# The passage from an 8-head into a 16-head attention: latents and first projections moved among the last heads, expert sums on GpSimd, row maxima subtracted with 64-row matmuls

## The chip, the cores and the metric

The kernel runs on one core of a Trainium2 chip. The time is device microseconds of the whole program, median of three runs, inputs in the chip's main memory at the start and the output there at the end. TensorE (PE) multiplies, VectorE (DVE), ScalarE (ACT) and GpSimd (POOL) do the elementwise work; each engine works off its own queue in order and they wait for one another on semaphores. Matrix products land in eight PSUM banks of 128 partitions by 512 floats; POOL does not touch them here.

## The reference, cut to what matters

```python
x = x + tanh(g_xattn[0]) * mlstm(layernorm(x), ctx)      # B=4, S=256, D=128
x = x + tanh(g_ffn[0]) * switch_head(layernorm(x))       # x2: 8 heads, 5 experts, 64 wide
x = x + tanh(g_xattn[1]) * L1_xattn(ctx, mask, layernorm(x))   # x3: 16 heads, 64 wide
x = x + tanh(g_ffn[1]) * experts(x)                      # 8 experts, best one

# end of switch_head: out is (b, t, 8, 64), md chooses 3 of 5 experts per head
o5 = einsum("bthd,dm->bthm", out, Wo).reshape(b, t, 8, 5, 128)
y = einsum("bthem,bthe->btm", o5, md)

# L1_xattn(features, masks, latents)
lat = layernorm(latents); kv = concat([layernorm(features), lat], 1)
q = lat @ Wq; k = kv @ Wk; v = kv @ Wv                    # 16 heads of 64, 512 keys
sim = (q * 64**-0.5) @ k.T; sim = sim - max(sim)
out = softmax(where(mask, sim, -inf)) @ v @ Wo
```

The kernel gathers `out` by expert first (`z`, 5 x 64 = 320 wide, the sum over heads of head output times md), and multiplies `z` by Wo: that gives x2. Latents are x2, normalized twice (once by the call, once inside).

## The kernel before

A batch is 256 rows, two tiles of 128; heads of the 8-head attention run in `pe_b`, `act_b`, `dve_b`, `pool_b`, heads of the 16-head attention in `pe_c`, `act_c`, `dve_c`, `pool_c`. A number is split into a high and a low fp16 half for most products, so a projection is three matmuls (high by high, high by low, low by high), the high half copied by ACT, the remainder subtracted by VectorE.

The 8-head attention has 12 steps per batch (`STEPS`), one head started in each of steps 0 to 7; steps 5 to 11 of batch b run in a loop together with the projections of batch b+1 (`Fori(0, B - 1)`). For the last batch steps 5 to 11 stand alone at the end. There `dve_b` adds statistics and norms of the latents of batches 0 to 2 (`latent_stats`, `latent_norm`, L688, L1851, L1855); then `copies_z` makes ten products of 512 (L775), POOL adds tile 0 over heads (L868 to L870) and VectorE tile 1 (L825 to L827), PE turns and multiplies z (L1712, L550), ACT copies it (L641, L642) and `add_x2` (L781) ends the stage. `latent_low` (L697, L699) and `latent_high` (L670) split the latents between. POOL meanwhile splits weight chunks (L1676 high, L1678 low).

The 16-head attention has 32 steps (`STEPS_C`), eight pairs of heads for each of four batches; a loop covers 24 of them. Step t on PE: `scores_T(t, 0)` (L1034, six pairs of 64-row matmuls of 256 columns; L1041 subtracts the maxima with a 128-row identity), `row_max(t+1, 0)` (L1019), job c, `scores_T(t, 1)`, `row_max(t+1, 1)`, jobs f and h, `values(t-1)` (48 matmuls, L1059 to L1061), and in two steps of a batch `project_ao` (L1067). ACT: the exponentials of a step (L1159 full, L1160 high half), job c's high copy after the first pair, f's and h's at the end (L1144). VectorE: `take_max` (L1250) for both halves with job c between, job f (L1241 for K), `take_out` (L1268, L1271), job h (L1239 for V). POOL: `low_exps` (L1361).

Jobs are the projections ahead: q in every other step at place c (L1244 its remainder), the turning of the finished output (ao) at c otherwise, K at f (L950 to L952), V at h. They take two PSUM banks in turns: a job waits until the job two before it is freed. `BEFORE` is the list of jobs ahead of step 0, `AFTER` the one behind step 31. The scores of a pair use banks 2 to 5; row maxima take banks 6 and 7, values and output bank 6 too:

```python
if n >= 2:
    pe.wait_ge(s.c_pj_free, it * PJ + (n - 1))          # job: two banks
...
if p >= 3:
    pe.wait_ge(s.c_O_free, it * HP2 + (p - 2))          # row_max(p, 0)
...
pe.wait_ge(s.c_max_done, it * PAIRS + (2 * t + 4))      # values(t-1) in step t
```

## Time and profile before

| | |
|---|---|
| time, median of 3 runs (lowest to highest) | 764.17 us (761.3 to 765.28) |
| profiled execution: time, span | 763.59 us, 761.9 us |
| busy, share of the span: PE, DVE, ACT, POOL | 80%, 75%, 43%, 55% |
| mean granted clock of TensorE | 0.880 |
| PE busy in tenths, slices 18 to 24 of 40 (19 us each, from 343 us) | 8 4 2 8 9 9 9 |
| chain that ended last | PE 57%, DVE 28%, issue 7%, ACT 3%, POOL 3% |

The shares are means over stages with different limits. What matters for a change in one stage are three views: the table of stretches (which engine is full there, and at which clock), the chain of waits in that stretch (which work ends last, piece by piece), and the timelines of the engines (how long one instruction takes, what it waited for; an idle time and its releaser stand in brackets).

### The profile page before, as it was taken

What the parts mean: (1) busy time and instruction counts of PE and PEld (TensorE: products, weight loads), DVE (VectorE), ACT (ScalarE), POOL (GpSimd) and SP (SyncE); (2) the same over time, 40 slices, a digit from 0 to 9 for tenths busy, and PEclk for the clock granted to TensorE, in tenths of its full rate; (3) what the DMA queues carried; (4) which work ended last, traced back from release to release, by engine and by line L of the source; (5) the groups of instructions that cost most, each with busy time, mean ns of one, the idle gap of its engine ahead of it and who ended that gap; (6) DMA issues with size and microseconds to landing.
All of it is one profiled execution on the core that took longest, in us unless ns stands there. A gap on an engine that the chain in (4) does not pass through costs nothing.

```text
span 761.9 us, 15577 instructions
## 1 busy us (share of the span) xinstructions
PE 610.9 (80%) x5721; PEld 387.8 (51%) x5721; DVE 569.0 (75%) x1043; ACT 324.3 (43%) x565; POOL 417.5 (55%) x349
## 2 busy tenths in 40 slices
PE   6399756798468658838428899999999998799997
PEld 5277522354244335325313456666666665566766
DVE  4837899659969985995976777667667766489887
ACT  2433200231132132113213787767858766455661
POOL 5424254417636652769593756656656666346652
PEclk9999977769779858965556999999999999989999
DMA  7311100000000000003310000000000000000001
GB/s 190 90 34 29 55 1 0 0 2 1 0 2 0 0 0 0 0 0 97 96 28 0 2 2 2 2 2 2 2 2 2 2 2 2 1 1 0 0 0 28
DMA packets 14163, 12.95 MB, mean 17 GB/s; under 512 B 3120, under 2 KB 11936, under 8 KB 14112
## 3 DMA queue, kind: packets, MB, share of 16 engines
q1 hardware_dynamic: 14112, 12.25, 5.6%
q8 instruction: 35, 0.57, 0.3%
q14 instruction: 16, 0.13, 0.1%
HBM read 11.72 MB, written 0.52 MB: 16 GB/s over the span
## 4 chain that ended last, share of the span: by engine, by line
PE 57%; DVE 28%; issue 7%; ACT 3%; POOL 3%; DVEq 1%; DMA 1%; ACTq 0%; SPq 0%; POOLq 0%; PEld 0%
DVE work L717 5%; PE banks L1034 5%; PE banks L1712 5%; DVE work L775 4%; PE banks L1041 4%; PE banks L950 3%; PE banks L465 3%; PE banks L1059 3%; PE banks L1019 2%; PE banks L952 2%; PE banks L951 2%; PE banks L1067 2%; PE banks L1422 2%; PE banks L1061 2%; PE banks L1060 2%
## 5 line engine op out<-in xcount | busy, mean ns | idle before, releaser
L1361 POOL TENSOR_TENSOR attn<-work,attn 128x512 f16<-128x512 f32 (+1 forms) x96 | 141.9, 1481 | 94.8 <-ACT attn L1160 94.8
L1250 DVE TENSOR_REDUCE nmax<-banks 128x2 bf16<-128x1024 f32 x64 | 78.3, 1223 | 21.5 <-PE banks L1019 21.3
L717 DVE TENSOR_TENSOR work<-banks,gatev 128x512 f32<-128x512 f32 x120 | 79.3, 684 | 15.8 <-PE banks L467 15.3
L465 PE MATMUL banks<-weights,xbTh 128*128 128x512 f16 x120 | 50.7, 422 | 28.2 <-DVE work L717 26.7
L1469 POOL TENSOR_SCALAR work<-work 128x512 f16<-128x512 f32 x64 | 53.0, 851 | 35.7 <-ACT work L1401 33.1
L1159 ACT ACTIVATE work<-banks,maskbias 128x512 f32<-128x512 f32 x64 | 44.3, 692 | 59.7 <-PE banks L1041 59.7
L845 POOL TENSOR_TENSOR work<-work 128x512 f32<-128x512 f32 x24 | 30.5, 1269 | 66.6 <-DVE work L717 64.6
L1407 DVE TENSOR_TENSOR work<-work 128x512 f16<-128x512 f32 x64 | 57.1, 949 | 12.2 <-POOL work L1469 12.2
L1712 PE MATMUL banks<-ident,work 128*128 128x128 f32 x276 | 53.3, 331 | 8.5 <-DVE work L1912 3.0
L490 PE MATMUL banks<-attn 64*128 64x256 f16 x64 | 22.1, 360 | 47.0 <-ACT work L631 37.9
L1059 PEld LDWEIGHTS banks<-work,attn 128*128 128x128 f16 x512 | 46.8, 97 | 18.8 <-POOL attn L1361 10.8
L1059 PE MATMUL banks<-work,attn 128*128 128x65 f16 x512 | 49.8, 193 | 5.2 <-DVE work L1271 2.5
L631 ACT ACTIVATE work<-banks,nm 128x256 f32<-128x256 f32 x64 | 26.7, 471 | 62.9 <-DVE nm L742 62.9
L1061 PE MATMUL banks<-work,attn 128*128 128x65 f16 x512 | 49.9, 193 | 0.0
L1060 PE MATMUL banks<-work,attn 128*128 128x65 f16 x512 | 49.9, 194 | 0.0
L466 PE MATMUL banks<-weights,xbTh 128*128 128x512 f16 x120 | 49.8, 415 | 0.0
L467 PE MATMUL banks<-weights,xbTl 128*128 128x512 f16 x120 | 49.8, 415 | 0.0
L1241 DVE TENSOR_TENSOR k2l<-banks,k2h 128x512 f16<-128x512 f32 x32 | 22.1, 692 | 36.0 <-ACT k2h L1144 36.0
L1712 PEld LDWEIGHTS banks<-ident,work 128*128 128x128 f32 x276 | 38.6, 170 | 19.6 <-issue 7.5
L1401 ACT ACTIVATE work<-banks,b1T 128x512 f32<-128x512 f32 x64 | 40.4, 688 | 15.6 <-PE banks L1395 15.5
L1061 PEld LDWEIGHTS banks<-work,attn 128*128 128x128 f16 x512 | 46.8, 98 | 0.0
L1060 PEld LDWEIGHTS banks<-work,attn 128*128 128x128 f16 x512 | 46.8, 97 | 0.0
(275 smaller groups left out, 1922.2 us busy)
## 6 DMA issues: line engine op xcount, KB each, us to landing
stage<-in_L_ffn_w SPq DMA_DIRECT2D x8, 512.0 KB, 3.9
stage<-in_L_ffn_Wkv SPq DMA_DIRECT2D x4, 640.0 KB, 3.9
stage<-in_L_ffn_Wq SPq DMA_DIRECT2D x2, 640.0 KB, 5.1
xt<-in_x SPq DMA_DIRECT2D x1, 512.0 KB, 4.2
ct<-in_ctx SPq DMA_DIRECT2D x1, 512.0 KB, 5.5
wo<-in_L_xattn_Wo SPq DMA_DIRECT2D x1, 512.0 KB
stage<-in_L_xattn_Wv SPq DMA_DIRECT2D x1, 512.0 KB, 3.7
stage<-in_L_xattn_Wq SPq DMA_DIRECT2D x1, 512.0 KB, 3.5
```

The lines of the kernel that those rows point to most:

```text
L465: pe.matmul(o, xh, wh, start=True, stop=False)
L466: pe.matmul(o, xh, wl, start=False, stop=False)
L467: pe.matmul(o, xl, wh, start=False, stop=True).then_inc(s.pj_ready, 1)
L717: dve.tensor_tensor(heads8(m.prod[:, k, e, :]), heads8(bank_pj[c % 2][:, :]), wide(g, DH1), ALU.mult).then_inc(s.prod_ready, 1)
L1059: pe.matmul(o, ph, vh, start=(kt == 0), stop=False)
L1060: pe.matmul(o, ph, vl, start=False, stop=False)
L1061: ins = pe.matmul(o, pl, vh, start=False, stop=(kt == KT - 1))
L1250: dve.tensor_reduce(m.nmax[:, p % 2, i, :], banks[:, 6:8, :], AX.X, ALU.max, negate=True).then_inc(s.c_max_done, 1)
L1361: pool.tensor_tensor(m.Pl[:, p % 2, kts, :], m.Pf[:, kts, :], m.Ph[:, p % 2, kts, :], ALU.subtract).then_inc(s.c_P_lo, 1)
L1407: dve.tensor_tensor(m.hTl[:, a, f, :], m.hf[:, use % HR, :], m.hTh[:, a, f, :], ALU.subtract).then_inc(s.h_lo, 1)
L1469: pool.tensor_scalar(m.hTh[:, use // FT, use % FT, :], m.hf[:, use % HR, :], 1.0, 0.0, ALU.mult, ALU.add).then_inc(s.h_hi, 1)
L1712: return pe.transpose(dst, src, m.ident[0:src.shape[0], 0:src.shape[0]])
```

## The change

- The loops of the 16-head attention are written out; `PJ` is 0 and a table `pj_no` counts the jobs.
- In `dve_b` the ten products and the sums of the last batch go. POOL makes them head by head (`z_head`): one product of both tiles and five experts, 640 elements, and one addition of 640, for heads 0 to 3 behind the batch loop and for heads 4 to 7 at steps 0, 2, 4 and 6.
- z of the last batch becomes ring jobs at place g: turned at steps 8 and 10 (zt), multiplied at 9 and 11 (zw), where VectorE adds x2.
- Latents are made batch by batch. Batch 0: statistics and norms behind head steps 5 to 7 of the last batch, its transposes are the first of the jobs `BEFORE`, which stand at head steps 8 to 11 (`TAIL`). Batches 1, 2, 3: statistics from steps 0, 4, 12, turned at g of steps 3, 7, 15, each with its valid keys behind.
- V tiles 0 and 1 of batch 0 are jobs at g of step 0 and at e of step 1. Order of the places is c, e, f, h, g.
- POOL's splits of w1 and w2 (eight chunks) go to steps 14 to 29, one half per step.
- The maxima are subtracted with 64-row matmuls of 128 columns in two passes; the second follows `row_max` and a wait for the first, and gives S_ready.

The diff, cut to its core:

```diff
+        def latent_stats(dve, stats, b, k):
+
+            if k == 0:
+                dve.wait_ge(s.x2_ready, I + b * I + I)
             else:
-                dve.wait_ge(s.x2n_ready, k)
-            src = m.ct if k % 2 else m.xt
-            stats(lambda t: src[:, tiles[t], :], len(tiles), m.st, m.mv, s.x2_var)
-
-        def latent_norm(dve, batches, k):
-            tiles = range(batches[0] * I, (batches[-1] + 1) * I)
-            src = m.ct if k % 2 else m.xt
-            dve.wait_ge(s.x2_var, k + 1)
-            dve.wait_ge(s.x2_rstd, k + 1)
-            for t in range(len(tiles)):
-                ins = dve.tensor_scalar(m.ct[:, tiles[t], :], src[:, tiles[t], :], m.mv[:, t, 0:1], m.rs[:, t:t + 1], ALU.subtract, ALU.mult)
...
-            z_group = SUMS + (B - 1) * GROUPS
-            for i in range(I):
-                copies_z(B - 1, i, z_group + i)
-
-            dve.wait_ge(s.z_ready, B * I)
-            t = m.prod[:, 1, :, :].rearrange("p e (h c) -> p e h c", h=H1)
-            ch.link(dve.tensor_tensor(t[:, :, 0:4, :], t[:, :, 0:4, :], t[:, :, 4:8, :], ALU.add))
-            ch.link(dve.tensor_tensor(t[:, :, 0:2, :], t[:, :, 0:2, :], t[:, :, 2:4, :], ALU.add))
-            dve.tensor_tensor(m.z[:, 1, :].rearrange("p (e c) -> p e c", e=E1), t[:, :, 0, :], t[:, :, 1, :], ALU.add).then_inc(s.z_last, 1)
...
+            def z_head(h):
+                if h == 0:
+                    pool.wait_ge(s.zT_ready, (B - 1) * I)
+                if h % 2 == 0:
+                    pool.wait_ge(s.O_free, (B - 1) * O1 + (h // 2 + 1 + RING))
+                heads = m.ho[:, :, h * DH1:(h + 1) * DH1].unsqueeze(2).to_broadcast([P, I, E1, DH1])
+                md = m.topm[:, (B - 1) * I:B * I, G1 + h * E1:G1 + (h + 1) * E1].unsqueeze(3).to_broadcast([P, I, E1, DH1])
+                dst = (m.z_head if h else m.z)[:, :, :].rearrange("p i (e c) -> p i e c", e=E1)
+                ch.link(pool.tensor_tensor(dst, heads, md, ALU.mult))
+                if h:
+                    ins = pool.tensor_tensor(m.z[:, :, :], m.z[:, :, :], m.z_head[:, :, :], ALU.add)
+                    if h < H1 - 1:
+                        ch.link(ins)
+                    else:
+                        ins.then_inc(s.z_sum, 1)
...
+            latent_rstd(0)
+            z_head(0)
+            latent_rstd(1)
+            for h in range(1, 4):
+                z_head(h)
+            return latent_rstd, z_head
...
+        PLACES = "cefhg"
+        LATENTS = {1: (0, 3), 2: (4, 7), 3: (12, 15)}
+        Z_AT = 8
...
+            if t < I:
+                jobs["ge"[t]] = ("v", 0, t, 0)
+            if Z_AT <= t < Z_AT + 4:
+                jobs["g"] = (("zt", "zw")[(t - Z_AT) % 2], B - 1, (t - Z_AT) // 2)
+            for lb, (_, at) in LATENTS.items():
+                if t == at:
+                    jobs["g"] = ("lat", lb)
...
-        BEFORE = [("q", 0, 0), ("v", 0, I, 0), ("k", 0, 0), ("k", 0, 1)] + [("v", 0, a, 0) for a in range(I)]
+        BEFORE = [("lat", 0), ("q", 0, 0), ("v", 0, I, 0), ("k", 0, 0), ("k", 0, 1)]
+        TAIL = {8: (0,), 9: (1,), 10: (2, 3), 11: (4,)}
...
+                elif kind == "zt":
+                    _, b, i = j
+                    pe.wait_ge(s.z_sum, b * I + 1)
+                    for c in range(3):
+                        w = min(P, E1 * DH1 - c * P)
+                        ins = turn(bank[0:w, c * P:(c + 1) * P], m.z[:, i, c * P:c * P + w])
+                    ins.then_inc(s.zT_ready, 1)
+                    return
...
-                for h in range(2):
-                    o = pair[h][:, :].rearrange("p (k i c) -> p k i c", k=2, i=I)
-                    for i in range(I):
-                        less = m.nmax[:, p % 2, i, h:h + 1].to_broadcast([P, P])
-                        ins = pe.matmul(o[:, :, i, :], less, m.identb[:, :].unsqueeze(1).to_broadcast([P, 2, P]), start=False, stop=(i == I - 1))
-                ins.then_inc(s.c_S_ready, 1)
+                less_max(p, half, 0)
...
+            def less_max(p, half, x):
+
+                pair = bank_kq[2 * half:2 * half + 2]
+                for i in range(I):
+                    for h in range(2):
+                        g = (x + h) % 2
+                        r = slice(DH2 * g, DH2 * g + DH2)
+                        o = pair[h][:, :].rearrange("p (k i c) -> p k i c", k=2, i=I)[:, :, i, r]
+                        ins = pe.matmul(o, m.nmax[r, p % 2, i, h:h + 1].to_broadcast([DH2, P]),
+                                        m.identb[r, r].unsqueeze(1).to_broadcast([DH2, 2, DH2]), start=False, stop=(x == 1 and i == I - 1))
+                        if x == 0 and i == I - 1:
+                            ins.then_inc(s.c_less_done, 1)
+                return ins
+
+            def rest_of_max(it, p, half):
+
+                pe.wait_ge(s.c_less_done, 2 * (it * PAIRS + (2 * p + half + 1)))
+                less_max(p, half, 1).then_inc(s.c_S_ready, 1)
...
                 scores_T(it, t, 0)
                 if t + 1 < STEPS_C:
                     row_max(it, t + 1, 0)
+                rest_of_max(it, t, 0)
                 if "c" in jobs:
                     job(it, (t, "c"), jobs["c"])
                 scores_T(it, t, 1)
                 if t + 1 < STEPS_C:
                     row_max(it, t + 1, 1)
-                for place in "fh":
+                rest_of_max(it, t, 1)
+                for place in "efhg":
...
+            def before(ps):
+                for p in ps:
+                    if p == 0:
+                        pe.wait_ge(s.x2_ready, I + (B - 1) * I)
+                        for n in range(N_W0, N_W1):
+                            pe.wait_ge(s.w_split, n + 1)
+                        pe.wait_ge(s.kv_free, 2)
+                    job(0, (-1, p), BEFORE[p])
...
+                if kind == "zt":
+                    dve.wait_ge(s.zT_copied, j[1] * I + (j[2] + 1))
+                    dve.wait_ge(s.c_pj_free, n)
+                    dve.sem_inc(s.c_pj_free, 1)
+                    return
...
+                for place in "hg":
+                    if place in jobs:
+                        low(it, (t, place), jobs[place])
+                for lb, (at, _) in LATENTS.items():
+                    if t in (at + 1, at + 2):
+                        latent_norm(dve, lb, t - at - 1)
+                    if t in (at, at + 1):
+                        latent_stats(dve, stats, lb, t - at)
...
+            tail[5] = lambda: latent_stats(dve, stats, 0, 0)
+
+            def second():
+                latent_norm(dve, 0, 0)
+                latent_stats(dve, stats, 0, 1)
+            tail[6] = second
+            tail[7] = lambda: latent_norm(dve, 0, 1)
...
+                if t in (0, 2, 4, 6):
+                    z_head(4 + t // 2)
+                if t == SPLITS_AT:
+                    pool.wait_ge(s.pj_ready, B * X1)
+                if SPLITS_AT <= t < SPLITS_AT + 2 * (N_WALL - N_W1):
+                    n, half = divmod(t - SPLITS_AT, 2)
+                    (split_low if half else split_high)(N_W1 + n)
```

## Rows read from the trace of the kernel before

**Rows 1.** Stretches: busy us (instructions) of PE, PEld, DVE, ACT, POOL; clock; DMA; GB/s.
```profile
180.00:200.00 20.00, 14.45 (x97) 7.18 (x97) 18.89 (x34) 2.28 (x4) 13.49 (x11) 1.00 0.00 1
340.00:360.00 20.00, 14.88 (x79) 10.25 (x79) 10.64 (x13) 6.22 (x17) 19.18 (x12) 0.50 0.25 79
...
380.00:400.00 20.00, 4.11 (x14) 2.75 (x14) 15.70 (x17) 1.94 (x6) 17.93 (x11) 0.50 0.10 27
...
460.00:480.00 20.00, 19.96 (x282) 12.47 (x280) 14.17 (x21) 16.19 (x27) 13.03 (x9) 1.00 0.01 2
```
**Rows 2.** Chain that ended last, 320 to 420 us: start, us, what.
```profile
378.08 6.12 DVE work L775 x10
384.22 4.06 DVE work L825
```
**Rows 3.** Timeline of VectorE: start us, us, engine, line, operation, out<-in, count [idle before <-releaser].
```profile
358.93 0.35 DVE L781 SCALAR_TENSOR_TENSOR xt<-banks,gf,xt 128x128 f32 x1 [3.06 <-PE banks L550]
...
373.36 4.06 DVE L688 TENSOR_SCALAR ct<-ct,mv,rs 128x128 f32<-128x128 f32 x6 [0.15 <-POOL rs L1648]
...
403.31 2.34 DVE L1256 COPY_PREDICATED kvTl<-masked,kvTl 128x256 f16<-128x256 uint8 x1
```
**Rows 4.** Timeline of ACT, the first exponential of the 16-head attention.
```profile
416.11 0.69 ACT L1159 ACTIVATE work<-banks,maskbias 128x512 f32<-128x512 f32 x1 [1.07 <-PE banks L1041]
```
**Rows 5.** Timeline of TensorE: the first scores of steps 0, 8 and 16.
```profile
414.33 0.39 PE L1034 MATMUL banks<-q2h,k2h 64*128 64x256 f16 x2
...
471.94 0.28 PE L1034 MATMUL banks<-q2h,k2h 64*128 64x256 f16 x2
...
531.24 0.28 PE L1034 MATMUL banks<-q2h,k2h 64*128 64x256 f16 x2
```
**Rows 6.** Timeline of POOL: sums over heads of a loop batch and of the last, a split.
```profile
342.94 1.86 POOL L869 TENSOR_TENSOR work<-work 128x640 f32<-128x640 f32 x1
...
359.29 1.04 POOL L1676 TENSOR_SCALAR weights<-stage 128x1024 f16<-128x1024 f32 x1
...
381.26 5.67 POOL L868 TENSOR_TENSOR work<-work 128x1280 f32<-128x1280 f32 x1 [4.68 <-DVE work L775]
```
**Rows 7.** Timeline of TensorE in one step, and the change L1019 to L1034 in step 30.
```profile
500.05 0.19 PE L1059 MATMUL banks<-work,attn 128*128 128x65 f16 x1
500.08 0.19 PE L1060 MATMUL banks<-work,attn 128*128 128x65 f16 x1
...
502.15 0.27 PE L1034 MATMUL banks<-q2l,k2h 64*128 64x256 f16 x2
502.35 0.61 PE L1041 MATMUL banks<-identb,nmax 128*128 128x256 bf16 x4
502.90 0.39 PE L1019 MATMUL banks<-k2h,q2h 64*128 64x512 f16 x2
503.22 0.28 PE L950 MATMUL banks<-kvTh,wq1h 128*128 128x256 f16 x1
...
637.25 0.39 PE L1019 MATMUL banks<-k2h,q2h 64*128 64x512 f16 x2
637.47 0.27 PE L1034 MATMUL banks<-q2h,k2h 64*128 64x256 f16 x2
```
**Rows 8.** Timeline of ACT: a step with an ao job (first two), one with a q job.
```profile
496.14 0.69 ACT L1159 ACTIVATE work<-banks,maskbias 128x512 f32<-128x512 f32 x1 [3.19 <-PE banks L1041]
...
500.24 0.64 ACT L1144 ACTIVATE k2h<-banks 128x512 f16<-128x512 f32 x1
...
503.00 0.69 ACT L1159 ACTIVATE work<-banks,maskbias 128x512 f32<-128x512 f32 x1 [1.64 <-PE banks L1041]
...
507.58 0.64 ACT L1144 ACTIVATE k2h<-banks 128x512 f16<-128x512 f32 x1
```
**Rows 9.** Timeline of VectorE: K's remainder, then take_out.
```profile
492.49 0.69 DVE L1241 TENSOR_TENSOR k2l<-banks,k2h 128x512 f16<-128x512 f32 x1 [1.32 <-ACT k2h L1144]
...
493.30 0.42 DVE L1271 TENSOR_TENSOR work<-banks,den 128x256 f32<-128x256 f32 x1
```

More of the change, by code:

```diff
@@ L661, in act_b @@
                 step(B - 1, h, False)
-                if h == STEPS - 1:
-                    for b in range(B - 1):
-                        latent_high(act, b)
-            for i in range(I):
-                copy_z(B - 1, i)
+                if h in tail:
+                    tail[h]()
         def latent_high(act, b):
@@ L932, in build @@
         for t in range(STEPS_C):
-            ordered += [((t, p), j) for p, j in c_jobs(t).items()]
+            ordered += [((t, p), j) for p, j in sorted(c_jobs(t).items(), key=lambda pj: PLACES.index(pj[0]))]
         ordered += [((STEPS_C, p), j) for p, j in enumerate(AFTER)]
         for place, j in ordered:
-            hi_no[place] = sum(1 for p in job_no if dict(ordered)[p][0] not in ("ao", "lat"))
+            hi_no[place] = sum(1 for p in job_no if dict(ordered)[p][0] in ("q", "k", "v", "norm"))
             job_no[place] = len(job_no)
@@ L940, in build @@
             if j[0] == "v":
-                v_no[j[1] * 2 + j[3]] = job_no[place]
-        PJ, PJ_HI = 3 * HP2, 3 * HP2 - 2 * I
-        for t in range(SPLIT_AT, STEPS_C - HP2 - 3):
-            assert all(job_no[t + HP2, p] == job_no[t, p] + PJ and hi_no[t + HP2, p] == hi_no[t, p] + PJ_HI for p in "cfh")
+                v_no[j[1] * 2 + j[3]] = max(job_no[place], v_no.get(j[1] * 2 + j[3], 0))
+        PJ, PJ_HI = 0, 0
+        pj_no = {place: sum(1 for q, j in ordered if job_no[q] < job_no[place] and j[0] not in ("zt", "zw")) for place in job_no}
         N_JOBS = len(job_no)
@@ L1281, in step @@
                     take_max(it, t + 1, 1)
-                if "f" in jobs:
-                    low(it, (t, "f"), jobs["f"])
+                for place in "ef":
+                    if place in jobs:
+                        low(it, (t, place), jobs[place])
                 if t >= 1:
@@ L1309, in dve_c @@
-            for it in range(B - 1):
-                for t in range(SPLIT_AT, SPLIT_AT + HP2):
-                    step(it, t)
-            for t in range(STEPS_C - HP2 + SPLIT_AT, STEPS_C):
+                for place in "hg":
+                    if place in jobs:
+                        low(it, (t, place), jobs[place])
+                for lb, (at, _) in LATENTS.items():
[3 more added lines that the diff above has]
+                        latent_stats(dve, stats, lb, t - at)
@@ new lines, in before @@
+            def before(ps):
+                for p in ps:
+                    if p == 0:
+                        dve.wait_ge(s.maskb_ready, 1)
+                        dve.wait_ge(s.v2_ones, 1)
+                        dve.wait_ge(s.tanh_ready, 1)
+                    low(0, (-1, p), BEFORE[p])
+            tail = {h: (lambda ps=ps: before(ps)) for h, ps in TAIL.items()}
+            tail[5] = lambda: latent_stats(dve, stats, 0, 0)
+            def second():
+                latent_norm(dve, 0, 0)
+                latent_stats(dve, stats, 0, 1)
@@ L1313, in dve_c, with run, attend16_dve @@
+            tail[6] = second
+            tail[7] = lambda: latent_norm(dve, 0, 1)
+            def run():
+                attend16_dve(dve, ch, norm, norm_stats, take_max, step, take_out, low, low_norm, add_x3)
+            return tail, run
+        def attend16_dve(dve, ch, norm, norm_stats, take_max, step, take_out, low, low_norm, add_x3):
+            dve.sem_inc(s.h_lo, HR)
+            for i in range(I):
+                take_max(0, 0, i)
+            for t in range(STEPS_C):
                 if t == STEPS_C - 1:
```

265 lines of the change are left out of this document (113 added, 152 removed).

## Prediction, made before any run of the changed kernel

> **What bounds the kernel now.** The view of stretches comes first, since the change lies between two stages with different limits. In the steady part of the 16-head attention TensorE is busy for 19.96 of 20 us at full clock [rows 1]; in the passage ahead of it TensorE works 4.11 of 20 us at half clock while VectorE is busy for 15.70 [rows 1]. The chain of waits, read second, says what the passage costs: it goes from work on VectorE to work on VectorE, through the ten products L775 and the sums from L825 on [rows 2], not through TensorE. The timelines give the rest. Last x2 of the batch loop at 358.93 [rows 3], first exponential of the 16-head attention at 416.11 [rows 4]: 57.2 us of passage. Then 32 steps of TensorE: step 0 starts at 414.33, step 8 at 471.94, step 16 at 531.24 [rows 5], so 57.6 us for steps 0 to 7 and 59.3 us for a batch of 8 later. The profiled execution took 763.59 us, 1.7 us over its span of 761.9, and lies 0.6 us under the median of 764.17; I work from 763.6.
>
> **Part 1, the passage.** Removed from it: ten products (6.12 us) and the first sum of tile 1 (4.06 us) with two smaller ones on VectorE [rows 2], three latents and two x2, after which the valid keys end only at 405.65 [rows 3], and the first projections behind them. The products and sums become 15 POOL instructions of 640 elements; L869, 640 elements wide, took 1.86 us [rows 6], so up to 3.6 us per head. They run beside the last heads and steps 0 to 6. What is late next is batch 0's own latent chain. From row to row (pieces without a group are my estimates from the same timelines, to 0.3 us each): VectorE ends head step 5 at 361.0 as now; statistics of two tiles 0.9 = 362.0; POOL's two instructions 1.1 = 363.1; norm and second statistics with head step 6's own work between, 2.5 = 365.6; head step 7, 1.9 = 367.5; last norm 1.4 (0.7 each beside POOL, L688 4.06 for six [rows 3]) = 368.9; transposes 0.8 = 369.7; latent_low with ACT's half 2.1 = 371.8; valid keys and head step 9 on VectorE 3.7 = 375.5 (one copy of them took 2.34 beside POOL's splits [rows 3], and POOL is now never idle there); low q, then V, K0 and K1, each three 512-column matmuls at half clock, about 1.3 us, plus copy and remainder on a ring of two banks = 381.2; two row maxima and the first scores 4.2 = 385.4. Against 416.1 that is **30.7 us won**. Ends: 34 (SBUF work of VectorE undisturbed by POOL) and 21 (every such instruction of POOL and VectorE stretched as at 381.26, where 1280 elements took 5.67 instead of 2.88 us [rows 6]). I take 30.7, since L699 and L1256 did stretch beside the splits and ops on PSUM did not. V tiles 0 and 1 are not removed but moved into steps 0 and 1.
>
> **Part 2, the maxima.** Each half of a step subtracts them now with four 256-column matmuls, one each 0.11 us, and around them lie changes between 64-row and 128-row work: L1034 ends and L1041 starts 0.20 us after the last pair instead of 0.11, L1019 to L950 is 0.32 for 0.213 of columns, while L1019 to L1034, both 64 rows, is 0.22 [rows 7]. So a change of row mode costs 0.09 to 0.11 us. The new form has eight 128-column matmuls in pairs: columns 0.44 to 0.22 per half and four changes of mode fewer per step. On TensorE that is 0.43 + 0.4 = 0.8 us per step. I don't take it, because TensorE would then no longer be the bound. What follows it is a chain that the change itself closes: S_ready is now given by rest_of_max, which stands *behind* row_max(t+1, 0) on TensorE, and that waits for take_out. Chain of a step: first exponential to the copy of K on ACT 4.58 us with a q job (503.00 to 507.58) or 4.10 with an ao job (496.14 to 500.24) [rows 8]; to its remainder L1241, 0.66; remainder to the end of take_out 1.23 (492.49 to 493.72) [rows 9]; then 0.06 to TensorE, row_max 0.213, rest_of_max 0.11 and 0.21 to its end and ACT. Sum 7.06 (q) and 6.58 (ao). Now these steps take 7.05 and 6.85. Steps with project_ao stay with TensorE: 8.91 now, 8.48 after (only columns and modes ahead of L1067 count). A batch of eight: 2 x 7.06 + 4 x 6.58 + 2 x 8.48 = 57.4 against 59.3: **1.9 us won per batch**, 3.8 for steps 16 to 31. Ends: 12.8 (0.8 in each of 16 steps, no chain) and a loss of 4.8 (0.3 per step, if the new wait shows). That wait is rest_of_max's for c_less_done; behind it on TensorE stand the c job and the second scores. It is covered by row_max, 0.213 us of columns, against the 0.2 us that a short matmul needs to its end (L1059, 0.19 [rows 7]); without that cover it costs up to 0.15.
>
> The Trainium skill has a rule against this part: TensorE: Matmul & The Clock Gate, LDWEIGHTS (loading the stationary operand), says that a load costs by its columns, not by its rows, some 107 ns for 128, so that eight loads of 64 rows cost twice four loads of 128. By it each half would cost 0.4 us more, not less. The trace doesn't bear it out here: L1059 and L1060, each with a 128-column load, follow at 0.03 us [rows 7].
>
> **Part 3, ring jobs.** The ring of projections has two banks, and job n waits until job n-2 is freed. With c, f, h that never hurts: h waits for c. A fourth job (g, or e at step 1) waits for f, the K projection. K's copy stands behind all exponentials on ACT, and its remainder ends 5.93 us after the first exponential (q) or 5.45 (ao). g stands ahead of values on TensorE, so values, scores and row_max wait. Counted from row_max0 (0.53 us before the first exponential): g starts at 6.52 or 6.04, then its own columns (zt 0.35, zw 0.65, lat 0.25, V 0.65), then 1.54 for values and 0.78 to the next row_max0 (1.87 more with project_ao). Steps: zt in q 9.2, zt with project_ao 11.1, zw in ao 9.0, lat 8.6, V at step 0 8.0 (no values) and 9.4 at step 1. There are nine of them: 0, 1, 3, 7, 8, 9, 10, 11, 15. Latents cost VectorE too: statistics and norm stand behind take_out and delay the next take_max0, 0.6 us per full pair and 0.4 otherwise; latent_low blocks ACT and VectorE after steps 3, 7 and 15, 1.4 us each. The z jobs add two waits on VectorE, for ACT's copy of zT and for the x2 it just wrote, with the next take_max0 behind; ACT has copied 1.2 us before that one is due, so nothing. Sum of steps 0 to 7: 8.0 + 9.4 + 7.7 + 8.7 + 8.5 + 7.0 + 7.7 + 8.7 = 65.7, against 57.6. Steps 8 to 15: 10.6 + 9.0 + 11.1 + 9.0 + 8.5 + 7.0 + 7.7 + 8.7 = 71.6 against 59.3. **Lost: 8.1 + 12.3 + 1.4 (step 16) = 21.8 us.** Bounds: zero, if K is freed before V's columns end, and 27, if all nine wait 0.6 us more. I take the rows' sum, since every link of it is a duration of the trace.
>
> POOL's splits of w1 and w2 go to steps 14 to 29: 1.04 us for a high half [rows 6] and twice that for a low one, beside 4.4 us of low_exps in steps of over 6.5; z_head, 3.6 us in every other step, fits in two steps too (8.9 + 3.6 + 1 under 14). Cover gone, each would cost about 1 us where it is late. Unrolled loops cost nothing: the steps outside the loop run at the same spacing. TensorE is idle in short pieces to 385, so step 0 runs at half clock longer than now; I add 1 us.
>
> Sum: 763.6 - 30.7 + 21.8 - 3.8 + 1 = 751.9.
>
> **Rivals.**
> A, forecast: 752, own range 743 to 760.
> B, the fourth job doesn't stop the ring: the nine waits (about 20 us together) go. 732, between 725 and 742. For it: TensorE waits nowhere for the ring now; against it: the order of the jobs in the code.
> C, TensorE's own rate rules, nothing waits: 763.6 - 30.7 - 32 x 0.8 + 6 of moved jobs = 713. Against it: ACT is busy 16.19 of 20 us [rows 1] and its chain has no slack for 0.8. The Trainium skill, TensorEngine Tiling (Array Packing), Key Properties, says that changing the tiling mode drains the engine, and by that rule alone C would come out; the 0.1 us of rows 7 agrees with the rule, not with the result.
> D, slower: TensorE's clock falls in steps 0 to 15. They leave TensorE idle for 2 us or more each, and 14.88 us of work in 20 stood at 0.50 once, though 14.45 stood at 1.00 elsewhere [rows 1]. At half clock values, scores, maxima and the extra job on the path cost some 2.3 us more per step: 16 steps give 37, so 788; it is slower from about six such steps on.
> E, the passage is stretched by POOL (z_head and VectorE at the slow end): 30.7 becomes 21, 762.
> F, loads set the pace of the 64-row maxima: 0.3 us per step on the chain, 32 steps, 762.
>
> **How the numbers follow.** A 0.50, B 0.20, C 0.06, D 0.10, E 0.08, F 0.06. Predicted 752. The range 729 to 767 holds A, E, F and most of B. 0.5% (3.8 us) is about what a measurement of this kernel can tell from no change. Faster by over that: A, B, C and a part of E and F, 0.78; within: the rest of E, F and A's upper tail, 0.12; slower: D, 0.10.
>
> **What would show it.** Right: the first exponential near 385; L1041's successor before row_max and behind it, 64 rows; in steps 8 to 11 a TensorE wait of 2 us for VectorE's K remainder just ahead of the z jobs; in steps 17 to 29 TensorE no longer full, its idle time ahead of row_max, released by take_out. Wrong: TensorE still at 20 of 20 us there with steps of 6.2 us (C), z jobs without a wait (B), a granted clock of 0.5 after 390 (D), or a first exponential past 392 (E).

## The result and the profile after

The changed kernel takes 768.28 us (median of 20 runs, 763.82 to 777.17) against 764.93 of the kernel before (20 runs beside them): a ratio of 1.0042, 95% interval 1.0023 to 1.0061. It is slower by 0.4%, where 752 was predicted with 729 as the low end and 767 as the high one; it lies 1.3 us past the high end. The profiled execution took 768.26 us with a span of 766.4; the mean granted clock is 0.893 against 0.880.

The span falls into four stretches, marked by the last x2 of the batch loop on VectorE, the first exponential of step 0 and that of step 31 on ACT. All tables below count this way, and a step lasts from its first exponential to that of the next one; x31 is the first exponential of step 31. Ratios are formed from fast runs alone and medians take in all of them; one profile per kernel is kept, and it need not stand at the median: those of e1 and e2 are of slow runs, 6 and 9 us above their medians, those of e7, e8 and e10 lie 6, 4 and 4 us above, that of e4 6.5 below.

| kernel | to last x2 | passage | steps 0-7 | 8-15 | 16-23 | 24-30 | behind x31 |
|---|---|---|---|---|---|---|---|
| before | 358.9 | 57.2 | 57.2 | 59.3 | 59.3 | 52.7 | 117.2 |
| after | 354.7 | 27.7 | 73.9 | 74.5 | 58.8 | 53.7 | 123.1 |

The passage gives 29.5 us, as foreseen; steps 0 to 15 take 31.9 more, the last stretch 5.9 more. What lies ahead of the passage is the same code in both; it varied from 353 to 364 us over the profiles of this study, with the granted clock in it, so its 4.2 us are not put down to the change. Counted from the last x2 to the end the two profiles take 403.0 and 411.7 us: the change costs 8.7 us there, more than the medians show. The first x2, the first exponential and the stretches that answer to [rows 1]:

```profile
354.74 0.35 DVE L752 SCALAR_TENSOR_TENSOR xt<-banks,gf,xt 128x128 f32 x1 [2.13 <-PE banks L547]
...
382.41 0.69 ACT L1176 ACTIVATE work<-banks,maskbias 128x512 f32<-128x512 f32 x1 [4.74 <-PE banks L1037]
```

```profile
360.00:380.00 20.00, 9.72 (x65) 4.97 (x67) 15.94 (x30) 4.71 (x10) 9.48 (x9) 0.66 0.00 1
384.00:404.00 20.00, 13.59 (x183) 8.13 (x178) 13.03 (x25) 14.44 (x23) 14.51 (x14) 1.00 0.00 1
404.00:424.00 20.00, 14.50 (x204) 9.63 (x203) 12.95 (x20) 11.23 (x19) 11.99 (x9) 0.83 0.01 2
560.00:580.00 20.00, 18.61 (x286) 12.95 (x283) 13.25 (x19) 15.40 (x24) 16.35 (x12) 1.00 0.15 42
```

TensorE, full for 19.96 of 20 us in the steady part before [rows 1], is busy for 13.6 and 14.5 in the first steps and for 18.6 even in steps 20 to 22. No engine is full in these rows: time went into waits. The timeline of TensorE shows them, idle time and releaser in brackets; shown are two waits of step 3, the last two z jobs (steps 10 and 11), and one of the quiet steps:

```profile
411.44 0.61 PE L1009 MATMUL banks<-k2h,q2h 64*128 64x512 f16 x2 [3.12 <-DVE nmax L1282]
415.52 0.69 PE L1759 MATMUL banks<-ident,ct 128*128 128x128 f32 x2 [0.58 <-DVE k2l L1273]
...
483.16 0.55 PE L1759 MATMUL banks<-ident,z 128*128 128x128 f32 x3 [2.51 <-DVE k2l L1273]
493.83 1.13 PE L980 MATMUL banks<-wo,zT 128*128 128x128 f32 x6 [2.32 <-DVE k2l L1273]
...
574.98 0.39 PE L1009 MATMUL banks<-k2h,q2h 64*128 64x512 f16 x2 [0.62 <-DVE work L1303]
```

The second to fourth are the ring: a fourth job waits for K's remainder (k2l). The last is the chain of part 2: row_max waits for take_out (work L1303). The first is neither; it waits for a maximum that VectorE gave late. The chain of waits in that stretch names the piece (start, us, what):

```profile
406.82 0.68 DVE work L1271
407.50 2.75 DVE ct L663 x2
410.25 1.14 DVE nmax L1282
411.44 0.61 PE banks L1009 x2
```

Two normalizations of 128 columns on VectorE take 2.75 us. Beside them, timeline of POOL and of VectorE, and the pair of one step earlier, of the first normalization:

```profile
407.30 1.26 POOL L837 TENSOR_TENSOR z_head<-work,topm 128x640 f32<-128x640 f32 x1
408.64 1.53 POOL L839 TENSOR_TENSOR z<-z,z_head 128x640 f32<-128x640 f32 x1
```

```profile
399.87 0.59 DVE L663 TENSOR_SCALAR ct<-xt,mv,rs 128x128 f32<-128x128 f32 x2
...
407.42 2.84 DVE L663 TENSOR_SCALAR ct<-ct,mv,rs 128x128 f32<-128x128 f32 x2
```

From 407.30 to 410.17 POOL makes a head of z; VectorE's pair ends at 410.26. At 399.87 POOL ends its subtractions (395.55, 4.35 us), and the pair takes 0.59.

### The profile page after: what moved, and what is told of

Same layout as the page of the kernel before. It is cut to its first block, busy times and chain, and to the rows that moved or that the text cites. A ratio compares the mean times of both kernels' runs of the same rounds, so it can differ in the third digit from the quotient of the medians.

```text
span 766.4 us, 16158 instructions
## 1 busy us (share of the span) xinstructions
PE 590.5 (77%) x5977; PEld 390.0 (51%) x5977; DVE 557.7 (73%) x1030; ACT 325.3 (42%) x565; POOL 428.7 (56%) x369
## 4 chain that ended last, share of the span: by engine, by line
PE 40%; DVE 34%; ACT 13%; issue 10%; POOL 1%; DVEq 1%; DMA 1%; ACTq 0%; SPq 0%; POOLq 0%; PEld 0%
DVE work L688 5%; ACT work L1176 4%; ACT attn L1177 4%; PE banks L1759 4%; DVE work L746 3%; DVE nmax L1282 3%; PE banks L465 2%; DVE k2l L1273 2%; PE banks L1463 2%; PE banks L1071 2%; PE banks L1464 2%; PE banks L1465 2%; DVE ct L663 2%; PE banks L467 2%; ACT k2h L1161 2%
## 5 line engine op out<-in xcount | busy, mean ns | idle before, releaser
L465 PE MATMUL banks<-weights,xbTh 128*128 128x512 f16 x120 | 49.5, 412 | 28.3 <-DVE work L688 26.4
L1448 DVE TENSOR_TENSOR work<-work 128x512 f16<-128x512 f32 x64 | 57.1, 949 | 13.1 <-POOL work L1510 13.1
L799 POOL TENSOR_TENSOR work<-work 128x512 f32<-128x512 f32 x24 | 30.5, 1269 | 63.4 <-DVE work L688 61.1
L1063 PE MATMUL banks<-work,attn 128*128 128x65 f16 x512 | 53.9, 199 | 6.8 <-DVE nmax L1282 3.8
L1063 PEld LDWEIGHTS banks<-work,attn 128*128 128x128 f16 x512 | 49.2, 101 | 15.7 <-POOL attn L1399 9.5
L1064 PE MATMUL banks<-work,attn 128*128 128x65 f16 x512 | 53.9, 199 | 0.0
L1065 PE MATMUL banks<-work,attn 128*128 128x65 f16 x512 | 53.8, 199 | 0.0
L1463 PE MATMUL banks<-weights,work 128*128 (+1 forms) x256 | 47.7, 229 | 3.0 <-DVEq L1513 2.9
L1064 PEld LDWEIGHTS banks<-work,attn 128*128 128x128 f16 x512 | 49.1, 101 | 0.2
L466 PE MATMUL banks<-weights,xbTh 128*128 128x512 f16 x120 | 49.2, 410 | 0.0
L1065 PEld LDWEIGHTS banks<-work,attn 128*128 128x128 f16 x512 | 49.1, 101 | 0.0
L1009 PE MATMUL banks<-k2h,q2h 64*128 64x512 f16 x128 | 25.7, 394 | 28.6 <-DVE nmax L1282 21.7
```

Of the source, the lines that this page charges most:

```text
L465: pe.matmul(o, xh, wh, start=True, stop=False)
L1063: pe.matmul(o, ph, vh, start=(kt == 0), stop=False)
L1064: pe.matmul(o, ph, vl, start=False, stop=False)
L1065: ins = pe.matmul(o, pl, vh, start=False, stop=(kt == KT - 1))
L1448: dve.tensor_tensor(m.hTl[:, a, f, :], m.hf[:, use % HR, :], m.hTh[:, a, f, :], ALU.subtract).then_inc(s.h_lo, 1)
L1463: pe.matmul(o, hh, m.w2h[:, e, f, :], start=(f == 0), stop=False)
```

## The experiments

All ratios are to the kernel before, run on the same chip in turns. The table gives every profile in the stretches of above. The last column, from the last x2 to the end of the program, is free of the varying stretch ahead (403.0 for the kernel before).

| kernel | median us | ratio, 95% interval | passage | 0-7 | 8-15 | 16-23 | 24-30 | behind x31 | x2 to end |
|---|---|---|---|---|---|---|---|---|---|
| after | 768.28 | 1.0042 (1.0023-1.0061) | 27.7 | 73.9 | 74.5 | 58.8 | 53.7 | 123.1 | 411.7 |
| e1 | 757.39 | 0.9877 (0.9791-0.9963) | 27.7 | 71.4 | 63.6 | 60.4 | 53.6 | 121.3 | 398.0 |
| e2 | 764.36 | 0.9997 (0.9956-1.0039) | 27.7 | 70.8 | 74.0 | 59.7 | 53.9 | 122.2 | 408.2 |
| e3 | 762.96 | 0.9972 (0.9932-1.0012) | 27.7 | 66.9 | 74.5 | 58.8 | 53.8 | 123.2 | 404.8 |
| e4 | 764.72 | 0.9993 (0.9953-1.0032) | 57.1 | 59.6 | 58.3 | 58.3 | 53.0 | 117.2 | 403.5 |
| e5 | 762.34 | 0.9983 (0.9957-1.0010) | 57.3 | 57.8 | 57.0 | 57.0 | 52.5 | 123.3 | 405.0 |
| e6 | 754.68 | 0.9897 (0.9859-0.9934) | 27.7 | 67.6 | 63.4 | 62.5 | 53.7 | 123.2 | 398.1 |
| e7 | 753.74 | 0.9834 (0.9787-0.9881) | 27.7 | 66.7 | 62.9 | 64.2 | 53.3 | 124.0 | 398.8 |
| e8 | 749.83 | 0.9733 (0.9692-0.9774) | 27.7 | 62.9 | 64.5 | 63.5 | 52.7 | 117.4 | 388.8 |
| e9 | 737.83 | 0.9643 (0.9600-0.9686) | 27.8 | 57.0 | 62.9 | 60.9 | 52.7 | 117.4 | 378.7 |
| e10 | 738.28 | 0.9635 (0.9607-0.9664) | 27.6 | 56.1 | 61.6 | 59.4 | 51.1 | 125.7 | 381.4 |
| e11 | 733.90 | 0.9596 (0.9539-0.9653) | 27.5 | 56.0 | 61.6 | 59.4 | 54.0 | 118.8 | 377.3 |
| e12 | 741.48 | 0.9732 (0.9676-0.9787) | 28.0 | 57.1 | 62.9 | 60.9 | 52.3 | 124.1 | 385.3 |

**e1: place g behind the values (on the changed kernel).**

```diff
-                for place in "efhg":
+                for place in "efh":
...
                     values(it, t - 1, t)
...
                     project_ao(it, n // 2 - 1, job_no[t - 1, "c"], bank_wo)
+                if "g" in jobs:
+                    job(it, (t, "g"), jobs["g"])
```

> The changed kernel with one edit: on TensorE the job at place g (V, lat, zt, zw of steps 0, 3, 7 to 11 and 15) is issued behind values and project_ao instead of ahead of them. The wait for K's remainder (6.0 to 6.5 us after the step's first row maximum) is then partly covered by values (1.54 us). Theory R (the two-bank ring stops values): steps 3, 7, 8, 9, 11 and 15 get 1.0 to 1.5 us shorter each, 7 to 10 us in all, and where TensorE's idle pieces get shorter the clock stays at full speed more often; 755 to 762. Theory N (the lost time is VectorE beside POOL and the clock alone): these steps keep their length, 766 to 770.

11 us under the changed kernel in the median, and 13.4 less in steps 0 to 15 (148.4 to 135.0). Behind the values K's remainder is there almost in time: the two multiplications of z still wait 0.86 us each, the first transposition 0.32, the second not at all, and steps 8 to 11 go from 9.79, 11.06, 11.15, 9.58 to 8.25, 7.84, 8.84, 7.84. The wait of the fourth job is real. But step 3 still lasts 12.07 us, and step 6 goes up from 9.59 to 12.14 while step 7 falls from 11.97 to 7.60: something else is there.

**e2: the changed kernel with the 128-row maxima of before.**

```diff
-                less_max(p, half, 0)
+                for h in range(2):
+                    o = pair[h][:, :].rearrange("p (k i c) -> p k i c", k=2, i=I)
+                    for i in range(I):
+                        less = m.nmax[:, p % 2, i, h:h + 1].to_broadcast([P, P])
+                        ins = pe.matmul(o[:, :, i, :], less, m.identb[:, :].unsqueeze(1).to_broadcast([P, 2, P]), start=False, stop=(i == I - 1))
+                ins.then_inc(s.c_S_ready, 1)
...
-                rest_of_max(it, t, 0)
...
-                rest_of_max(it, t, 1)
```

> The changed kernel with the maxima subtracted as before: four 128-row matmuls of 256 columns, S_ready ahead of row_max, no second pass. Theory S (the new form closes a chain through take_out, so that TensorE's saved 0.8 us is not paid out): steps without project_ao return to 7.05 and 6.85 from 7.2 and 6.7, steps with it from 8.52 to 8.9; in all 0 to 5 us slower than the changed kernel, 768 to 773. Theory C (the 64-row form is worth its TensorE time, 0.8 us per step): 20 us slower, 785 and above.

The 64-row form brings nothing here: without it the kernel is 3 to 4 us faster, where 0 to 5 us slower was forecast, by ratios whose intervals overlap, though quiet batches are shorter with it. Of the profile only the quiet steps are read here: 7.04, 6.85 and 8.91 against 7.2, 6.71 and 8.53.

**e3: POOL leaves out heads 4 to 7 of z; x2 of the last batch is summed from heads 0 to 3 alone.**

```diff
             def z_head(h):
+                if h >= 4:
+                    if h == H1 - 1:
+                        pool.sem_inc(s.z_sum, 1)
+                    return
```

> The changed kernel with POOL's products and additions of heads 4 to 7 at steps 0, 2, 4 and 6 left out (z then holds heads 0 to 3 only; the output lacks their part). Theory P (VectorE's norm instructions stand still beside POOL's float32 work, 2.8 instead of 0.6 us at steps 2, 5 and 6, and TensorE's idle time behind them costs its clock): steps 3, 6 and 7 get 2 to 4 us shorter each, 6 to 9 us in all, 758 to 763. Theory Q (these steps are long because of the ring alone): less than 1 us in all.

Step 3 goes from 12.76 to 10.21, step 6 from 9.59 to 7.54, step 7 from 11.97 to 9.59; no other step changes by over 0.1. That is 7.0 us for work that is beside the path. VectorE's pairs of normalizations:

```profile
407.40 0.59 DVE L663 TENSOR_SCALAR ct<-ct,mv,rs 128x128 f32<-128x128 f32 x2
432.00 0.59 DVE L663 TENSOR_SCALAR ct<-xt,mv,rs 128x128 f32<-128x128 f32 x2
439.54 0.59 DVE L663 TENSOR_SCALAR ct<-ct,mv,rs 128x128 f32<-128x128 f32 x2
```

In the changed kernel these three took 2.84, 2.63 and 2.83. The Trainium skill, SBUF — State Buffer (Who interferes with whom), says that VectorE and GpSimd share one pair of ports as an exclusive lock, so that one blocks for the whole of the other's instruction; this holds for VectorE instructions that use both ports for one operand or read two operands from SBUF. The rows agree: normalizations (SBUF to SBUF) went from 0.59 to 2.8, while the subtractions that read a PSUM bank (L1271) stay at 0.68 or 0.69 beside POOL.

**e4: the kernel before with the 64-row maxima (the second pass behind row_max, as in the change).**

```diff
                 if t + 1 < STEPS_C:
                     row_max(it, t + 1, 0)
+                rest_of_max(it, t, 0)
...
                     row_max(it, t + 1, 1)
+                rest_of_max(it, t, 1)
```

> The kernel before with one part of the change alone: the 64-row maxima in two passes, S_ready from the second, behind row_max. Theory S (a chain exponentials, K's copy and remainder, take_out, row_max, S_ready bounds the steps): steps of 7.1 to 7.2 (q), 6.6 to 6.7 (ao) and 8.5 us (with project_ao), 1.5 to 2 us per batch of eight, 6 to 8 us in all: 757 to 760. Theory C (TensorE's time is paid out): 0.7 to 0.8 us in each of 32 steps, 739 to 743. Theory W (the wait for the first pass shows on TensorE): no gain or a loss, 765 and above.

Part 2 alone is worth nothing that can be measured: 764.72 against 764.06, where 757 to 760 was forecast. Quiet steps are 7.19, 6.70 and 8.53, a batch 58.3 instead of 59.3, and TensorE is no longer full (18.37 of 20 us where before it was 19.96 [rows 1]):

```profile
540.00:560.00 20.00, 18.37 (x277) 12.79 (x272) 14.09 (x22) 14.23 (x24) 11.62 (x8) 1.00 0.01 2
```

It loses it again in steps 0 to 7 (59.6 against 57.2) and in step 30 (8.64 against 7.33). Step 30 has a granted clock of 0.80 where the kernel before has 1.00; of the 2.3 us in steps 0 to 7, 1.0 is in step 0 at an undiminished clock and 0.65 in step 1 at one of 0.81.

**e5: e4 with the second pass ahead of row_max.**

```diff
+                rest_of_max(it, t, 0)
                 if t + 1 < STEPS_C:
                     row_max(it, t + 1, 0)
-                rest_of_max(it, t, 0)
```

> The kernel before with the 64-row maxima, as in e4, but with the second pair of each half (rest_of_max, which gives S_ready) ahead of row_max on TensorE instead of behind it. Theory S: in e4 the steps of 7.2 and 6.7 us are set by S_ready standing behind row_max, which waits for the copy of K, its remainder and take_out; without that the steps fall to what TensorE needs, 0.8 us of saved columns and mode changes less about 0.3 for the wait on c_less_done that now lies open: 6.6 (q), 6.4 (ao), 8.4 (project_ao), a batch of eight at 55.6 instead of 58.3, three batches 8 us, so about 756 against e4's 764.7. Rival T: the wait on c_less_done costs 0.2 us per half and the exponentials still follow row_max one step later (the maxima of the next step need it), so steps stay within 0.1 us of e4's, 764, or grow to 59.5 per batch, 768.

Quiet steps fall to 6.73, 6.6 and 8.6, a batch to 57.0 (expected 55.6), TensorE is at 19.43 of 20:

```profile
540.00:560.00 20.00, 19.43 (x284) 13.17 (x281) 14.37 (x22) 14.40 (x24) 11.74 (x9) 1.00 0.01 2
```

So the chain through take_out was closed by where S_ready stood, and the wait on c_less_done, open now, costs less than the chain did. Of the 4.8 us that the steps gain against e4, the stretch behind step 31 takes 6.1 back in this profile, and the medians differ by 2; the forecast was 8.

**e6: the fourth jobs at a place d right behind c.** POOL's heads 4 to 7 move to steps 0, 3, 7, 8, the z jobs to 10 to 13, the last latents to step 16.

```diff
-        PLACES = "cefhg"
-        LATENTS = {1: (0, 3), 2: (4, 7), 3: (12, 15)}
-        Z_AT = 8
+        PLACES = "cdfh"
+        LATENTS = {1: (0, 3), 2: (4, 7), 3: (13, 16)}
+        Z_AT = 10
...
-                jobs["ge"[t]] = ("v", 0, t, 0)
+                jobs["d"] = ("v", 0, t, 0)
...
-                if "c" in jobs:
-                    job(it, (t, "c"), jobs["c"])
+                for place in "cd":
+                    if place in jobs:
+                        job(it, (t, place), jobs[place])
```

> The changed kernel with its fourth ring jobs (V tiles 0 and 1, latents, transposes and projections of z) issued right behind job c, ahead of the second scores, instead of behind f or h: then d waits for the h job of the step before and f waits for c, which were freed long ago. POOL's products of heads 4 to 7 go to steps 0, 3, 7 and 8, away from VectorE's norms, the z jobs to steps 10 to 13, the last latents to step 16 and the copies of valid keys behind job h. Theory (the ring's wait for K's remainder and the norms beside POOL are what the steps 0 to 15 lost): waits of 2 us ahead of the extra jobs gone; steps 0 to 15 at 7.2, 6.7 and 8.5 with 1 us more at the three latents: 56 + 59 + 3 = 118 instead of 148 us, so the kernel at 738 to 742. Rival (a lowered clock and ACT's and VectorE's own time for the extra jobs keep what was lost): steps 0 to 15 at 133 or more, the kernel at 753 or more.

The steps with z jobs are 8.75, 6.99, 8.76 and 6.99 instead of 9.79, 11.06, 11.15 and 9.58: four z jobs cost 1.0 us over quiet steps where they cost 12.4. Steps 8 to 15 gain 11 us. The kernel is at 754.7, though, and steps 0 to 15 at 131, not 118, between the two forecasts: steps 2, 4, 8 and 16 are 10.4 to 11.9 us long. They follow normalizations and copies of valid keys beside POOL (2.40 us for a pair at 396.36).

**e7: e6 and e5's order of the maxima.** Diff as e5 on e6.

> e6 and e5's order of the maxima together. By theory S another 8 to 10 us below e6, some 731; by rival T as e6 or up to 5 us above it.

1 us under e6 in the median, where 8 to 10 us were forecast. Its quiet steps are those of e5, but steps 16 and 17 are 10.3 and 10.2 and the last stretch is 124.0.

**e8: e6 with the 128-row maxima.** Diff as e2 on e6.

> e6 with the 128-row maxima of the kernel before (S_ready ahead of row_max, four matmuls of 256 columns per half). Nominal steps 7.05, 6.85 and 8.91 instead of 7.2, 6.7 and 8.53: 0.5 to 1 us more per batch of eight, 2 to 4 us above e6, if the maxima only move the nominal steps; equal to e6 or up to 4 us below it if, as e2 against the changed kernel suggested, the new form loses more in disturbed steps than it wins in quiet ones.

5 us *below* e6, against what quiet steps say. The gain is in steps 0 to 7 (62.9 against 67.6) and behind step 31 (117.4 against 123.2). From the last x2 to the end it is 9.3 us; this profile has 363.6 us ahead of the passage, e6's 354.4, so the medians may show too little of it. This profile shows the lock at its plainest; timeline of VectorE and, under it, of POOL:

```profile
405.46 2.79 DVE L663 TENSOR_SCALAR ct<-xt,mv,rs 128x128 f32<-128x128 f32 x2
...
415.06 0.59 DVE L663 TENSOR_SCALAR ct<-ct,mv,rs 128x128 f32<-128x128 f32 x2
...
422.95 1.43 DVE L1275 COPY_PREDICATED kvTh<-masked,kvTh 128x256 f16<-128x256 uint8 x1
424.30 1.75 DVE L1275 COPY_PREDICATED kvTl<-masked,kvTl 128x256 f16<-128x256 uint8 x1
```

```profile
404.93 3.23 POOL L1388 TENSOR_TENSOR attn<-work,attn 128x512 f16<-128x512 f32 x2
...
422.84 1.26 POOL L837 TENSOR_TENSOR z_head<-work,topm 128x640 f32<-128x640 f32 x1
424.18 1.60 POOL L839 TENSOR_TENSOR z<-z,z_head 128x640 f32<-128x640 f32 x1
```

The pair at 405.46 ends at 408.25, when POOL's two subtractions have ended at 408.16. It isn't z_head alone: POOL's subtractions stand beside a slow normalization as well. What puts them there is POOL's work ahead of them. At 405.46 that was its two small instructions for rstd and a head of z, at 518.62 (2.88 us for the pair) the same two and a split of weights; where the two for rstd alone came first (409.47 and 440.53) POOL was done in time and the pairs took 0.59.

**e9: e8 with POOL's extra work away from those places.**

```diff
-        LATENTS = {1: (0, 3), 2: (4, 7), 3: (13, 16)}
-        Z_AT = 10
+        LATENTS = {1: (0, 3), 2: (9, 12), 3: (14, 17)}
+        Z_AT = (9, 10, 11, 13)
...
-        SPLITS_AT = 14
+        SPLITS = (8, 8, 13, 13) + tuple(range(18, 30))
...
-                if t in (0, 3, 7, 8):
-                    z_head(4 + (0, 3, 7, 8).index(t))
+                if 4 <= t < 8:
+                    z_head(t)
```

> e8 (extra ring jobs behind c, 128-row maxima) with POOL's extra work moved away from the steps in which VectorE normalizes latents or copies valid keys: heads 4 to 7 of z in steps 4 to 7, latents of batch 2 from step 9 (transposed in 12), of batch 3 from 14 (in 17), z jobs in steps 9, 10, 11 and 13, two of the splits each in steps 8 and 13, the rest in 18 to 29. In e8's trace the pairs of normalizations took 2.79 us (405.46) and 2.88 (518.62) beside POOL's subtractions and products and 0.59 where POOL was idle (415.06), and the two copies of valid keys 3.2 us beside POOL against 0.8. Theory (VectorE's SBUF-to-SBUF instructions stand still while POOL runs an f32 tensor_tensor): those durations go back to 0.59 and 0.42 each, about 2.2 us in each of four or five steps, some 10 us: 740, between 737 and 744. Rival (the steps of 9 us and more have another cause, the extra job or ACT's wait for the latents): within 2 us of e8, 748 or more.

All six pairs for batches 1 to 3 take 0.59 or 0.60, all copies of valid keys 0.42. Steps 0 to 7 fall from 62.9 to 57.0, the whole to 737.8, 3.6% under the kernel before. In e8 steps 2, 4, 8 and 16 held a slow pair or a slow copy and lasted 9.60, 9.41, 9.41 and 10.65 us; here they last 7.42, 7.12, 7.06 and 7.43. That is 10.0 of the 10.1 us that all steps gain, although z jobs and latents moved too. The same latents that made step 3 of the changed kernel 12.76 us long are in a step of 7.40 here, and TensorE in the first steps:

```profile
384.00:404.00 20.00, 18.64 (x186) 9.93 (x186) 14.23 (x26) 14.62 (x24) 10.44 (x10) 0.91 0.01 1
404.00:424.00 20.00, 19.07 (x265) 11.79 (x266) 14.90 (x27) 15.12 (x24) 14.08 (x11) 1.00 0.01 2
```

**e10: e9 with e5's maxima.** Diff as e5 on e9.

> e9 with the 64-row maxima and both pairs ahead of row_max, as in e5 and e7. Nominal steps by e5: 6.73 (q), 6.6 (ao), 8.6 (project_ao), a batch of eight 57.0 instead of 59.3. If that holds in all 32 steps: 7 to 9 us below e9, about 733. If, as between e8 and e7, the form with 64 rows gives it back in the disturbed steps and behind step 31 (123 to 124 us there in e5 and e7, 117.4 in e8): within 3 us of e9.

The steps are 5.5 us shorter in all (228.1 against 233.6), the stretch behind step 31 is 8.3 us longer, the median is 738.3: nothing won. From the last x2 to the end the profiles differ by 2.7. What the two do there, TensorE alone (stretch, length, busy, instructions, clock, DMA); first e9, x31 at 620.75, then e10, x31 at 614.83:

```profile
620.75:624.25 3.50, 2.45 (x26) 1.00 0.00 0
624.25:627.75 3.50, 2.01 (x63) 1.00 0.00 0
627.75:631.25 3.50, 2.32 (x50) 1.00 0.02 5
631.25:634.75 3.50, 3.50 (x31) 1.00 0.00 0
```

```profile
614.83:618.33 3.50, 1.70 (x24) 1.00 0.00 0
618.33:621.83 3.50, 3.12 (x54) 0.74 0.00 0
621.83:625.33 3.50, 2.67 (x49) 0.50 0.02 5
625.33:628.83 3.50, 2.67 (x14) 0.50 0.00 0
```

The work behind step 31 starts at 2.4 GHz in both; in e10 it falls to 1.2 GHz in the second 3.5 us (0.74 in the mean, then 0.50), in e9 it doesn't until 638.

**e11 and e12: the two forms by step.** e11 has the 64-row form of e10 in steps 0 to 23 and the 128-row form from 24 on; e12 the other way round.

```diff
+        NEW_MAX = lambda t: t < 24
...
+                if NEW_MAX(p):
+                    less_max(p, half, 0)
+                    return
...
             def rest_of_max(it, p, half):
+                if not NEW_MAX(p):
+                    return
```

> e10 with the 64-row maxima in steps 0 to 23 alone and the 128-row form in steps 24 to 31. The question is the stretch behind step 31: 117.4 us in before, e8 and e9, 121 to 126 in after, e1, e2, e3, e5, e6, e7 and e10, but 117.2 in e4. Theory U (the less full steps 24 to 31 of the new form are what makes the clock fall behind step 31): steps 0 to 23 as in e10, 24 to 30 back at 52.7, behind step 31 117 to 119, median 734. Rival V (it hangs on when the idle pieces there come relative to the clock's changes, and differs from kernel to kernel and run to run): the median is 1.6 us above e10 or within 2 us of it, 738 to 741, and the stretch may be either length.

> The mirror of e11: 128-row maxima in steps 0 to 23 as in e9, the 64-row form with both pairs ahead of row_max in steps 24 to 31. Theory U: steps 24 to 30 at 51.1 instead of 52.7 and the stretch behind step 31 at 123 to 126 instead of 117.4: median 741 to 744, above e9's 737.8. Rival V: 736 to 738, and the stretch may be either length.

733.9 and 741.5 us, with 118.8 and 124.1 behind step 31: theory U's medians and stretches on both sides. Steps 24 to 30 missed its numbers by 1.3 and 1.2 us (54.0 and 52.3), in step 30 alone: it lasts 8.61 and 8.69 us at a mean clock of 0.80 and 0.82, against 7.32 and 7.42 at 1.00 in e9 and e10. e11 has the lowest median of the study, 4.0% under the kernel before (interval of the ratio 0.9539 to 0.9653), but its interval overlaps those of e9 and e10; the one of e12 lies above it and touches that of e9. U isn't a full account: e4 has the 64-row form in all steps and 117.2, e2 the 128-row form and 122.2. In all profiles the clock falls somewhere in that stretch; what differs is how often and over which work. That the form of the maxima in the last steps, through TensorE's idle time, is one of the things that move it is likely by e9 to e12 and not shown, with one profile of each and rival V open.

## Why the prediction was wrong, point by point

Predicted 751.9, profiled 768.3. The difference by stretches: ahead of the passage -4.2 (the same code), passage +1.2, steps 0 to 7 +8.2 against the step times and -1 for the clock term, which was taken by itself, steps 8 to 15 +2.9, steps 16 to 23 0, steps 24 to 30 +2.9 (53.7 against 50.8), behind step 31 +5.9; the last 0.5 is rounding, the time outside the span and where steps are counted from.

**Passage: right, with its links.** 26.5 us from the last x2 to the first exponential were worked out, 27.7 measured. The last normalization ends 10.8 us behind x2 (10.0 worked out), the latent's remainder 14.0 (12.9), K1's remainder 23.7 (22.3). The pair of norms took 2.39 instead of 1.4 and the copies of valid keys 3.0 beside POOL; since POOL's sums hide beside the last heads, rival E (762) is out.

**Part 2: mechanism right, two sizes off, and what follows from it missed.** TensorE isn't full and row_max waits for take_out by 0.62 us in the quiet steps, as foretold. Steps came out at 7.2 (q), 6.71 (ao) and 8.53 (project_ao) for 7.06, 6.58 and 8.48, so a batch of 58.3 for 57.4: half of the 1.9 us that was forecast per batch. e5 shows the other half of the reasoning, that without the order TensorE would be the bound again. Steps 24 to 30 missed by 2.9: 2.3 of it is step 30 (9.38 us, 7.06 by the sum), the rest the two sizes. In step 30 the sum had no term for the clock, whose mean there is 0.64. It is 1.00 in the profiles in which that step lasts 7.3 or 7.4 us (before, e8, e9, e10) and 0.80 to 0.82 in five in which it lasts 8.5 to 8.9 (e2, e4, e5, e11, e12), and both forms of the maxima are in either group. On the whole the part was by e2 a loss of 3 to 4 us instead of a gain of 3.8, with intervals that overlap, and in the kernel before nothing (e4). That a TensorE with idle time loses its clock more easily is the likely reason, argued from these and not shown. Rival C is out (steps of 6.2 us never came), and so is F: with the chain opened (e5) eight short matmuls with their loads take less time than four long ones.

**Part 3, ring: mechanism right.** "In steps 8 to 11 a TensorE wait of 2 us for VectorE's K remainder just ahead of the z jobs" is what the rows show (2.51 and 2.32). Steps 8 to 11 were put at 10.6, 9.0, 11.1, 9.0 and are 9.79, 11.06, 11.15, 9.58, step 9 with a clock of 0.85; 0 and 1 at 8.0 and 9.4 and are 8.19 and 9.45. Rival B is out. e6 shows that the price was one of order, not of work.

**Part 3, POOL: the failed step.** "z_head, 3.6 us in every other step, fits in two steps too" counts POOL's time and not what POOL does to VectorE. The passage's bound did weigh just that ("every such instruction of POOL and VectorE stretched"), and the splits of [rows 3] (4.06 for six norms, 2.34 for one copy) showed it; for steps 0 to 15 "0.6 us per full pair" was taken, the undisturbed time. Measured: 7.0 us in steps 3, 6 and 7 (e3), of the 16.4 by which the time was missed, and 10.1 from e8 to e9, where all such meetings of the steps go. Without the 7.0 the time would have been inside the range.

**Clock: rival D in part.** Step 3 holds 5.98 us of TensorE's work at a clock of 0.54, behind 3.1 us of idle time; the clock is 0.85 and 0.84 in two more stretches. Granted levels, TensorE alone:

```profile
404.00:411.00 7.00, 4.23 (x89) 0.97 0.01 2
411.00:418.00 7.00, 5.98 (x59) 0.54 0.00 0
444.00:450.00 6.00, 3.57 (x35) 0.85 0.00 1
466.00:477.00 11.00, 8.75 (x110) 0.84 0.01 1
```

D had it from the ring's waits in all 16 steps; it came in three steps of the sixteen: 3 and 7, behind a meeting of VectorE with POOL, and 9, behind the ring's wait. With z_head gone (e3) step 7 is at 1.00, step 3 still at 0.83 instead of 0.73 and step 9 unchanged at 0.85; with shorter waits of the ring (e1) step 9 is at 1.00; with both gone (e9) all three are. The term of +1 us was too small for steps 0 to 7; how much of the 7.0 us of e3 is clock and how much VectorE isn't parted by these runs, since one brings the other.

**Behind step 31: a term put at nothing.** The sum has no term for that stretch. Its code is the same, and still 5.9 us of the 16.4 were lost there, by the clock; what makes the clock fall more often is open.

**The range.** It covered the slow ends one at a time. E or F alone gave 762. What came was the meetings with POOL (7.0 us), the stretch behind step 31 (5.9) and step 30 (2.3) at once; no rival held any of the three, so that 767 was nearly reached is no merit of the range.

## What to carry to other kernels

When work moves to GpSimd, list the VectorE instructions that will run beside it and that read and write SBUF alone: each may last as long as GpSimd's (normalizations and predicated copies did here), and what stands behind it on VectorE holds up TensorE. Put an extra job into a ring where the bank that it takes was freed long ago, and give a semaphore ahead of whatever waits. A saving on a full engine may buy idle time only: ask what the clock does with it, and measure the stretch behind as well. Where one profile per kernel is kept, compare it from a mark behind the part that varies by itself.
